# A linear-attention block with a mixture of experts on one core: the second half's state of each chunk is summed at the end of the values' visit

## The reference

```python
q, k = lrpe(silu(x @ Wq)), lrpe(silu(x @ Wk))       # 16 heads, 8 features each, doubled to 16 by cos and sin
energy = einsum('bhnd,bhmd->bhnm', q, k) * tril(ones(n, n))
out = einsum('bhnm,bhmd->bhnd', energy, v)
x = layernorm(x + norm((out @ Wo) * sigmoid(x @ G1 @ G2)))
x = layernorm(x + shared_ffn(x) + routed_experts(x))
```

## Time and profile before

| | |
|---|---|
| median of 3 runs | 820.63 us (820.49 to 820.79) |
| span of the profiled execution, first to last instruction | 819.0 us |
| outside the span, against the median | 1.6 us |
| PE busy | 771.5 us (94%) |
| DVE busy | 583.9 us (71%) |
| ACT / POOL busy | 368.2 us (45%) / 415.7 us (51%) |
| mean granted TensorE clock | 0.988 of full speed |
| share of PE in the chain of waits that ended last | 78%, DVE 10% |

### The profile page before, as it was taken

One profiled execution on the slowest core, in us unless ns is written; L12 is line 12 of the kernel. 1 busy time (PEld: TensorE's weight loads), 2 busy tenths in 40 slices (PEclk: granted clock), 3 DMA queues, 4 the chain that ended last, 5 costly groups with the idle time before them and its releaser, 6 DMA issues.

```text
span 819.0 us, 30731 instructions
## 1 busy us (share of the span) xinstructions
PE 771.5 (94%) x12462; PEld 627.2 (77%) x12462; DVE 583.9 (71%) x1865; ACT 368.2 (45%) x802; POOL 415.7 (51%) x395
## 2 busy tenths in 40 slices
PE   5889999999999999999998889899999999999994
PEld 4667777777777777778776677688999989899884
DVE  7488798888888888898868898845444454544674
ACT  6334564646546465564633332223322333323484
POOL 6441243523435243342534555671677778876442
PEclk9999999999999999999999999999999999999997
DMA  4155233231333323233322212114444455433455
GB/s 148 46 174 180 78 92 85 64 93 53 100 76 78 90 57 97 61 86 77 77 64 54 69 34 70 42 53 137 98 87 58 80 98 102 72 52 42 126 151 145
DMA packets 71163, 70.56 MB, mean 86 GB/s; under 512 B 11443, under 2 KB 54250, under 8 KB 71024
## 3 DMA queue, kind: packets, MB, share of 16 engines
q1 hardware_dynamic: 53928, 52.33, 23.2%
q0 software_dynamic: 17024, 16.28, 11.0%
q10 hardware_dynamic: 72, 0.00, 0.0%
HBM read 23.99 MB, written 28.89 MB: 65 GB/s over the span
## 4 chain that ended last, share of the span: by engine, by line
PE 78%; DVE 10%; issue 4%; DMA 3%; SPq 2%; POOL 2%; ACT 1%; POOLq 0%; DVEq 0%; ACTq 0%
PE energy_banks L1935 5%; PE bank L1853 5%; PE energy_and_gate_banks L1853 5%; PE bank L1855 5%; PE bank L1854 5%; PE energy_and_gate_banks L2409 4%; PE bank L2409 4%; PE energy_and_gate_banks L1960 4%; PE energy_and_gate_banks L1855 3%; PE energy_and_gate_banks L1854 3%; PE bank L1894 3%; PE energy_banks L1853 3%; PE energy_banks L1855 3%; PE energy_banks L1854 3%; PE bank L1895 2%
## 5 line engine op out<-in xcount | busy, mean ns | idle before, releaser
L626 POOL DMA_INDIRECT dispatched_rows<-x,slot x128 | 140.0, 1093 | 224.5 <-PE energy_banks L1935 132.4
L760 POOL DMA_INDIRECT summed_rows<-VP,goal_i x80 | 123.8, 1548 | 42.5 <-issue 22.7
L1119 ACT ACTIVATE sq<-energy_banks 128x512 f32<-128x512 f32 (+1 forms) x96 | 50.5, 526 | 120.2 <-PE energy_banks L1855 118.5
L842 ACT ACTIVATE hidden_rounded<-sf 128x512 fp32r<-128x512 f32 x88 | 55.3, 628 | 58.8 <-DVE sf L1273 58.0
L832 ACT ACTIVATE sf<-energy_and_gate_banks 128x512 f32<-128x512 f32 x88 | 52.4, 596 | 62.2 <-PE energy_and_gate_banks L1855 60.8
L1273 DVE TENSOR_TENSOR sf<-sf,bank 128x512 f32<-128x512 f32 x88 | 60.1, 683 | 19.4 <-PE bank L1855 19.2
L1935 PE MATMUL energy_banks<-EM,VP 64*32 64x64 f32 x4096 | 59.1, 225 | 1.1 <-issue 1.1
L1243 DVE TENSOR_TENSOR EM<-energy_and_gate_banks,causal 128x512 f32<-128x512 f32 x64 | 43.9, 686 | 18.7 <-PE energy_banks L1960 18.7
L1853 PE MATMUL energy_and_gate_banks<-xgT_hi,ws_hi 128*128 128x512 f32 x108 | 52.1, 482 | 3.4 <-DVE EM L1243 2.6
L1935 PEld LDWEIGHTS energy_banks<-EM,VP 64*32 64x32 f32 x4096 | 47.8, 105 | 4.2 <-issue 3.2
L1853 PE MATMUL bank<-xgT_hi,ws_hi 128*128 128x512 f32 x108 | 45.9, 425 | 3.7 <-DVE sf L1273 1.4
(11 more groups left out here) (255 smaller groups left out, 2178.4 us busy)
## 6 DMA issues: line engine op xcount, KB each, us to landing
QM<-QT SPq DMA_DIRECT2D x248, 32.0 KB
dispatched_rows<-empty POOLq DMA_DIRECT2D x8, 655.0 KB
QM<-dispatched_rows SPq DMA_DIRECT2D x8, 655.0 KB, 6.2
QT<-sq SPq DMA_DIRECT2D x40, 128.0 KB
KT<-sq SPq DMA_DIRECT2D x40, 128.0 KB
xin<-in_x SPq DMA_DIRECT2D x16, 256.0 KB, 2.9
QM<-summed_rows SPq DMA_DIRECT2D x16, 256.0 KB, 2.8
out_x<-QM SPq DMA_DIRECT2D x16, 256.0 KB, 3.2
```

Source lines behind the costliest of these rows:

```text
L626: g.indirect_dma_start(out=xg_d, out_offset=bass.IndirectOffsetOnAxis(ap=slot[:, n % 2, j:j + 1], axis=0), in_=x1[:, n % 2, j % NC, :], in ...
L760: g.indirect_dma_start(out=sum_d, out_offset=bass.IndirectOffsetOnAxis(ap=goal_i[:, par, t:t + 1], axis=0), in_=ye[:, par, t, :], in_offse ...
L842: a.activation(hs_hi[:, f], sf[:, n % SF], ACT.Copy).then_inc(a_hh, 1)
```

## The change

`state(c, 1)` leaves the end of the energies' visit and comes to the end of the values' visit, directly behind `attend` of chunk c-1. On DVE, the copies of odd steps (k = 1, 3, 5) move one place up, ahead of the masking of the same chunk's energies instead of behind it. All else stays, the semaphores and their values too. There are three such states in each of the 16 blocks (the fourth chunk has none), 48 in all.

```diff
@@ DVE, with_feed_forward; the same in the other four orders @@
                     shared_hidden(b, 0)
+                    mask_state(b, 3)
                     mask(b, par, 1)
-                    mask_state(b, 3)
                     hidden_lo(b, 0)
...
                     shared_hidden(b, 2)
+                    mask_state(b, 5)
                     mask(b, par, 2)
-                    mask_state(b, 5)
                     hidden_lo(b, 1)
...
@@ PE @@
-                def states_and_out(c):
+                def both_states_and_out(c):
...
                         attend(b, par, c - 1)
                     elif c == 0 and back:
                         attend(b - 1, 1 - par, 3)
-
-                def energies_and_state(c):
+                    if core:
+                        state(c, 1)
+
+                def energies_alone(c):
 
                     if core:
                         energies(c)
-                        state(c, 1)
...
-                    states_and_out(2)
+                    both_states_and_out(2)
                     shared_gate(2)
                     shared_up(2)
-                    energies_and_state(2)
+                    energies_alone(2)
```

More of the change, by code:

```diff
@@ L2090, in first_blocks @@
                         input_turned()
-                    states_and_out(0)
+                    both_states_and_out(0)
                     project(f, 0)
-                    energies_and_state(0)
+                    energies_alone(0)
                     if back:
@@ L2115, in with_feed_forward @@
                         input_turned()
-                        states_and_out(0)
+                        both_states_and_out(0)
                         project(f, 0)
-                        energies_and_state(0)
+                        energies_alone(0)
                         turn_x1(b, par)
-                        states_and_out(1)
+                        both_states_and_out(1)
                     else:
-                        states_and_out(0)
+                        both_states_and_out(0)
                         down_by_column(shared_turn(b - 1), range(3))
@@ L2133, in with_feed_forward @@
                     shared_up(0)
-                    energies_and_state(1)
+                    energies_alone(1)
                     project_out(b)
                     shared_pair(1)
-                    states_and_out(2)
+                    both_states_and_out(2)
                     shared_gate(2)
                     shared_up(2)
-                    energies_and_state(2)
+                    energies_alone(2)
                     values_projected(0)
@@ L2192, in with_spare_pairs @@
                         shared_up(s1, SPARE)
-                        states_and_out(2)
+                        both_states_and_out(2)
                         logits(b)
                         project(f, 2)
-                        energies_and_state(2)
+                        energies_alone(2)
                         project(f, 3)
                         values_projected(0)
-                        states_and_out(3)
+                        both_states_and_out(3)
                         values_projected(1)
-                    energies_and_state(3)
+                    energies_alone(3)
                     keys_turned()
```

60 lines of the change are left out of this document (30 added, 30 removed).

## The result

The changed kernel takes 839.6 us (median; 836.4 to 842.5) against 820.6 before: 1.0224 times as long, 95% interval 1.0195 to 1.0254. The forecast was 830.3 with a range of 822.5 to 834.5. So the direction was right, the loss, 19 us, is twice the one worked out, and the time lies above the range. The span of the profiled execution grew from 819.0 to 837.5, by 18.5.

A forecast was written before the change was run, and what follows sets the result against it. The prediction took PE to bound blocks 3 to 11 (busy 336.37 of 339 us). Terms 3.2 + 3.2 + 2.1 + 1.2 = +9.7 us on the 819.0 span gave 828.7, plus 1.6 for the median: 830.3 us, range 822.5 to 834.5.

The forecast's parts named there:

- PE saves 0.26 at the energies: Third energies to dense matmul: 0.20 us without the state instead of 0.46, at 48 places, 12.5 us saved.
- If all copies are in time, the change gives -5.8 us: All 48 moved states: 12.5 us saved at the energies, 6.7 paid behind the values, with no wait for copies.
- rival A: All blocks: DVE's copies are in time, only -5.8 us is left, 814.8 us; chance 0.08.
- Blocks 3 to 11, +0.35 each: Third visit's state waits for DVE's copy of step 4: +0.35 us per block, +3.2 in nine blocks.
- Blocks 12 to 14 and 15, +1.05 each and +2.1: Late copies: first visit in 12 to 14 (+3.2 us together, read from block 13), second visit in 15.
- Less 0.26 at the energies: Block 15: 0.26 us saved at the energies, taken off the delay to give +2.1.
- Blocks 0 to 2, I take 0.4: First three blocks: 0.4 us each, chosen between 0 and block 13's 1.05, +1.2 us together.
- What costs nothing: POOL: POOL's waits for summed states and attended chunks, now found together, cost nothing; PE does not wait for its sends in stage 1.
- Rival C, the clock: New PE waits bring two or three more lowered-clock stretches, about 1.7 us each: 834.3 us; chance 0.10.

The follow-up runs named there:

- two: Kernel before, with the change only in the first two visits of blocks 3 to 11: 820.3 us, 1.0002.
- prompt: Kernel before, with the change in blocks 3 to 11 and DVE's copy of step 4 ahead of the second pair's hidden values: 819.5 us, 0.9994.
- steady: Kernel before, with the change on PE and DVE only in blocks 3 to 11: 823.2 us, 1.0025.
- filled: Changed kernel plus 1 to 7 identity matmuls in front of the second states with the longest stops: 840.9 us, 1.0258.
- timely: Changed kernel, with DVE's late even copies put sooner in DVE's order in all blocks: 831.9 us, 1.0138.
- ends: Kernel before, with the change only in blocks 0 to 2 and 12 to 15: 835.8 us, 1.0195.
- split: Kernel before, with the change in blocks 0 to 2 and 12 to 15, but the state behind the first large matmuls after the values: 830.2 us, 1.0108.
- after_sh32: Changed kernel plus 32 tiny matmuls in the opening of PE's program: 843.5 us, 1.0251.

## Why the prediction was right in its direction and wrong in its size

*PE saves 0.26 at the energies*: the step is there, at another place than the prediction says. What it calls the third energies of block 9, 303.63, is the end of the first visit; the third ends at 320.05, and there the step is 0.46 too. In block 9 after, the last energies of the first visit start at 311.50 and the dense matmul at 311.71:

```profile
311.50 0.27 PE L1960 MATMUL energy_banks<-QM,KT 32*64 32x128 f32 x2
311.71 0.50 PE L1894 MATMUL bank<-hidden_rounded,sd_hi 128*128 128x512 f32 x1
```

*If all copies are in time, the change gives -5.8 us*: wrong. two and prompt have the copies in time and gain nothing clear of the noise. I took PE's busy share (336.37 of 339 us) for a bound by PE. In prompt a PE that is earlier waits for DVE's masks a little further on (the 1.7 us in seven of the nine blocks); that a round of PE, DVE and ACT sets the block's length is how I read this, not a thing that a run isolates. The step of 0.21 without the state against 0.46 with it agrees with a cost at each change of tile. The Trainium skill, "TensorEngine Tiling (Array Packing)", Key Properties, has a change of the tiling mode drain TensorE. What that rule alone would make of the time fell with rival A.

*Blocks 3 to 11, +0.35 each*: right; 2.5 / 9 = 0.28, with the stop at the third visit and its +0.61. steady repeats it alone.

*Blocks 12 to 14 and 15, +1.05 each and +2.1*: this step failed by its size, 5.3 against 10.0. The mechanism, a late copy whose delay is passed on, is right in block 13. By the ends of the fourth energies' visits (before 431.25, 456.88, 481.55 and 504.47, after 441.40, 468.62, 496.85 and 523.55), block 12 grew by 1.2, block 13 by 1.6, block 14 by 3.6 and block 15 by 3.8. One block stood for three, and only one late copy was priced in each; all four have two stops for copies: 0.53 and 0.93 us in block 12 (not at the first visit), 0.95 and 0.57 in 13, 0.98 and 0.53 in 14, 0.77 and 0.93 in 15. Besides there are what the sum had no term for: program stops of 1.33 and 0.67 in blocks 13 and 14, and three lowered stretches against two, two of them in blocks 14 and 15. How the missing 4.7 us splits among these is not shown. *Less 0.26 at the energies* in block 15 is the smaller fault: in block 13, where I looked, the gate waits for masks, and the state had been free in that wait (the rows at 444 and 456 us above).

*Blocks 0 to 2, I take 0.4*: this step failed too. I had no row for it and set it near nothing; 6.4 us came in the one profile, with stops for copies of 0.35, 1.28, 0.39 and 1.69 (3.7 together), a program stop of 3.05 in block 1 of which about half is lost (a kind that the prediction does not have at all), and stretches of lowered clock at 20 and 79 us. Single profiles spread by up to 4 us here, so the size of the miss is rough.

*What costs nothing: POOL*: neither shown nor refuted; three pairs of runs differ by +2 to -5, within their intervals.

*Rival C, the clock*: the stretches came, three more, as it said; by the repeated runs about 3.4 of the 19 us, at most 5.1 in the profile. It is not the main cause: filled had fewer of them and was no faster. The Trainium skill, "TensorE: Matmul & The Clock Gate", Part 1, says that an idle array falls to half its clock. The stops of PE in front of the six stretches agree.

What the 19 us are made of, then: 7.7 for late copies (shown by timely) and, as an estimate, about 3.4 for the clock, which timely does not give back (0.983 on average). Some 8 are left. The runs show that most of the loss sits at the ends (ends), and that a loss is left there without late copies and without the long run behind the values (split). How much of them is plain delay of the masks and how much program stops (6.7 us in the profile of timely, some 2 in that of the kernel before) stays open, and so does why the orders tried at the ends stop more for their program than the order before.

## What to carry to other kernels

A busy share of 99% does not make an engine the bound: before counting a saving, look for the wait that comes next, and whether the moved work was free inside a wait where it stood. Work behind a link of a chain can be free; the same work ahead of that link delays all that follows. And a stage for which no row was read should go into the range with its upper bound, not into the sum near zero, nor should the one block that was read stand for its neighbours.

## What the hardware showed that I had not expected

PE stopped for 0.7 to 4.0 us inside a run of small matmuls or right behind it, with no engine to wait for, and went on some 1.2 to 1.6 us behind the landing of a 16 KB packet of its program queue. Shortly before two such packets other DMA queues were busy for over 90% of the time, at others they were not: from 499.5 to 501.0 us in after_sh32, in front of a stop of 2.17 whose packet started at 500.5, the busiest queue had 26%, and in steady, in front of the stop of 2.34, no transfer at all started from 25.0 to the packet at 27.7. So other transfers are not needed for such a stop.
